# A second feed-forward bias as one more row of the down projection, with a new order table for the layers

## The reference

```python
xn = _layernorm(x)
x = x + _L0_attn_ref(xn, ...) + _L0_ffn_ref(xn, ...)

def _layer(x, wqkv, qs, ksc, wo, lg, lb, w1, b1, w2, b2):   # two of these, one after the other
    h = shift_token(x)                # second half of the columns comes from the token before
    ...                               # q, k, v; l2 norm; rotary tables; windowed attention
    x = x + o @ wo
    h = shift_token(x)
    h = (h - mu) / jnp.sqrt(var + 1e-05) * lg + lb
    h = h @ w1 + b1                   # 256 -> 2 * 682
    a, g = jnp.split(h, 2, axis=-1)
    h = a * jax.nn.gelu(g, approximate=False)
    x = x + h @ w2 + b2               # 682 -> 256; b2 is the bias that the change moves
    return x
```

## Time and profile before

| | us |
|---|---|
| three runs | 1958.6, 1950.5, 1962.69 |
| median | 1958.6 |
| the profiled execution | 1963.61 |
| its span, first to last instruction | 1961.8 |
| TensorE busy (matmul) | 1842.9, 94% of the span |
| ScalarE / VectorE / GpSimd busy | 1376.9 / 1246.3 / 922.5 |
| mean granted TensorE clock | 0.981 |

### The profile page before, as it was taken

The page is one execution under the profiler, slowest core; times in us unless marked ns, Lnnn a source line. Parts: engine busy times, 40 slices in busy tenths (PEclk is TensorE's granted clock), DMA queues, the critical chain, the costliest instruction groups (busy, mean ns, idle before and its releaser), DMA issues.

```text
span 1961.8 us, 47822 instructions
## 1 busy us (share of the span) xinstructions
PE 1842.9 (94%) x17808; PEld 1567.0 (80%) x17808; DVE 1246.3 (64%) x4125; ACT 1376.9 (70%) x3997; POOL 922.5 (47%) x1315
## 2 busy tenths in 40 slices
PE   6999999999999689999999999999999999999998
PEld 4788788788788469788788897887888878878777
DVE  4544543454443367777777777677777777777765
ACT  5886987878688365866757758667576585775764
POOL 2533543444344454636536446355364563654632
PEclk9999999999999889999999999999999999999999
DMA  4321320322324610110110101304112112010110
GB/s 146 99 76 56 116 87 34 116 76 77 88 78 146 196 41 23 47 55 23 47 43 24 55 15 53 122 15 166 39 39 63 34 47 65 25 54 25 44 45 28
DMA packets 127003, 128.91 MB, mean 66 GB/s; under 512 B 28112, under 2 KB 101940, under 8 KB 126772
## 3 DMA queue, kind: packets, MB, share of 16 engines
q1 hardware_dynamic: 123604, 119.56, 19.7%
q10 hardware_dynamic: 3168, 6.29, 0.9%
HBM read 72.84 MB, written 37.25 MB: 56 GB/s over the span
## 4 chain that ended last, share of the span: by engine, by line
PE 41%; DVE 11%; ACT 11%; issue 1%; POOL 1%; DMA 1%; SPq 0%; DVEq 0%; ACTq 0%; POOLq 0%
PE f_bank L1415 17%; PE f_bank L1552 7%; PE f_o_bank L1527 4%; PE f_scores L1567 4%; PE f_scores L1494 3%; ACT f_prob L1649 3%; DVE f_u L1803 3%; DVE f_gu L1799 2%; PE f_bank L1505 2%; ACT f_u L1669 2%; PE f_bank L1466 2%; PE f_bank L1509 1%; ACT f_probT L1590 1%; DVE f_actT L1688 1%; ACT f_probT L1594 1%
## 5 line engine op out<-in xcount | busy, mean ns | idle before, releaser
L594 POOL TENSOR_SCALAR a_prob<-a_prob,a_row_inv,a_gate 128x128 f32<-128x128 f32 x512 | 227.6, 468 | 377.7 <-DVE a_row_inv L932 377.7
L1370 POOL TENSOR_SCALAR f_prob<-f_prob,f_row_inv 128x192 f32<-128x192 f32 x512 | 214.5, 443 | 291.6 <-DVE f_row_inv L1745 291.6
L1415 PE MATMUL f_bank<-weights,f_actT 128*128 128x512 f32 x1152 | 302.9, 409 | 5.4 <-DVE f_norm L1693 3.9
L1552 PE MATMUL f_bank<-f_hT,f_w 128*128 128x256 f32 x2112 | 270.2, 283 | 5.4 <-DVE f_gu L1799 5.4
L1552 PEld LDWEIGHTS f_bank<-f_hT,f_w 128*128 128x128 f32 x2112 | 259.4, 189 | 10.3 <-DVE f_gu L1799 8.9
L1415 PEld LDWEIGHTS f_bank<-weights,f_actT 128*128 128x128 f32 x1152 | 211.7, 193 | 55.4 <-DVE f_norm L1693 7.7
L1352 POOL TENSOR_TENSOR f_qk_tok<-f_qk_tok,tables 128x512 f32<-128x512 f32 x128 | 165.1, 1313 | 158.4 <-DVE f_sin_part L1705 158.4
L1649 ACT ACTIVATE f_prob<-f_scores,f_neg_max 128x192 f32<-128x192 f32 x512 | 208.5, 428 | 14.1 <-DVE f_neg_max L1737 12.8
L1346 POOL TENSOR_TENSOR f_norm<-f_norm,f_minus_half 128x16 f32<-128x16 f32 x64 | 199.3, 3115 | 34.0 <-DVE f_norm L1697 32.4
L1669 ACT ACTIVATE f_u<-f_gu 128x256 fp32r<-128x256 f32 x192 | 80.3, 418 | 191.2 <-DVE f_gu L1799 191.2
L824 ACT ACTIVATE a_prob<-a_scores,a_neg_max 128x128 f32<-128x128 f32 x512 | 179.9, 392 | 24.0 <-DVE a_neg_max L923 17.0
(11 more groups left out here) (139 smaller groups left out, 3988.8 us busy)
## 6 DMA issues: line engine op xcount, KB each, us to landing
split_weights<-a_hi_lo SPq DMA_DIRECT2D x16, 512.0 KB
x_next<-states SPq DMA_DIRECT2D x32, 256.0 KB, 4.4
tables<-scaled_tables SPq DMA_DIRECT2D x16, 512.0 KB, 5.4
f_x<-states SPq DMA_DIRECT2D x16, 512.0 KB, 3.8
split_weights<-a_hi_lo SPq DMA_DIRECT2D x12, 682.0 KB
weights<-split_weights ACTq DMA_DIRECT2D x6, 1024.0 KB, 9.9
f_w<-split_weights SPq DMA_DIRECT2D x4, 1280.0 KB, 10.6
f_v_crossed<-f_v SPq DMA_DIRECT2D x40, 128.0 KB, 2.3
```

The costliest lines, as they stand in the source:

```text
L594: last = nc.gpsimd.tensor_scalar(part, part, row_inv[:, a % 2, head, t:t + 1], gate[:, half, t, h:h + 1], ALU.mult, ALU.mult)
L1370: last = nc.gpsimd.tensor_scalar(part, part, row_inv[:, a % 2, head, t:t + 1], 1.0, ALU.mult, ALU.mult)
L1415: last = nc.tensor.matmul(out, lhs(c, a), rhs(c, b), start=(i == 0), stop=(i == len(order) - 1))
L1552: mm = nc.tensor.matmul(out[:, which * PART:(which + 1) * PART], w1[:, wp, c, col:col + P], hT[:, hp, c, columns_of(a // FH)], start=(i == ...
```

## The change

The bias b2 becomes row 43 of the last block (`HR = HL + 1`). Its weight row in w2 is b2 itself, as high and low part. Its activation is 1: the gate's bias in that row is 8 (`UNIT_GATE`), whose gelu is 8, and the value's bias is 1/8. Both constants are written into `rows` by memsets. The steps `x1_bias` go, on GpSimd and in the semaphores. b2 is split in the attention phase (one ScalarE and one VectorE instruction on a tile of 2 x 512, a load and a store). `ORDER` is another table, in which also `load_x` stands ahead of `load_x1`, and `load_wqkv` after `("rope", 3)` and not at the end. The attention phase's last iteration has no `rows_in` and `rows_out` any more. The bookkeeping of semaphore values is written anew (`Count`), and TensorE waits for weights only where they are new.

```diff
+HR = HL + 1
+UNIT_GATE = 8.0
 # attention phase
         last = [(kind, a) for kind, a in steps if not (kind in A_PREPARE and a == HALVES - 1 or ...)
+                and kind not in ("rows_in", "rows_out")]
 # SP
+            sp.dma_start(bias[:], rows_in[2]).then_inc(bias_loaded, 16)
...
+                        if it == 0:
+                            sp.wait_ge(bias_split, 1)
+                            sp.dma_start(split_bias, bias_hi_lo[:].bitcast(F32)).then_inc(bias_stored, 16)
 # GpSimd
-            pool.memset(rows[:], 0.0)
+            gate_col, value_col = 3 * D + FH - 1, ROWS - 1
+            pool.memset(rows[:, 0:gate_col], 0.0)
+            pool.memset(rows[:, gate_col:gate_col + 1], 1.0 / UNIT_GATE)
+            pool.memset(rows[:, gate_col + 1:value_col], 0.0)
+            pool.memset(rows[:, value_col:ROWS], UNIT_GATE)
 # ScalarE and VectorE, once (it == 0 and a == 0)
+                            act.wait_ge(bias_loaded, 16)
+                            nc.scalar.activation(bias_hi_lo[:, HI, :], bias[:], ACT.Copy).then_inc(bias_hi, 1)
...
+                            nc.vector.tensor_tensor(bias_hi_lo[:, LO, :], bias[:], bias_hi_lo[:, HI, :].bitcast(F32), ALU.subtract).then_inc(bias_split, 1)
 # layers phase, the table (two of its lines)
-ORDER = [("softmax", 0), ("scores", 0), ("scores", 1), ("weigh", 0), ("weigh", 1), ("softmax", 1), ("load_x1", 0), ("transpose_x", 0),
...
+ORDER = [("softmax", 0), ("softmax", 1), ("scores", 0), ("scores", 1), ("weigh", 0), ("scores", 2), ("weigh", 1), ("transpose_x", 0),
...
+                sp.dma_start(w2[HL:HR, :, FH - 1, :].bitcast(F32), bias_in[layer].unsqueeze(0)).then_inc(w2_loaded, 16)
 # GpSimd
-                    elif kind == "x1_bias":
-
-                        pool.wait_ge(ln_scaled.sem, ln_scaled.past(it, ("ln_apply", 2 * a + 1)))
...
-                        nc.gpsimd.tensor_tensor(x1[:], x1[:], b2_row.unsqueeze(1).broadcast_to([P, TILES, D]), ALU.add).then_inc(x1_biased.sem, 1)
...
+                    pool.wait_ge(ln_scaled.sem, ln_scaled.past(it, ("ln_apply", 2 * a + 1)))
 # TensorE, prepare()
                     if a % TILES == 0:
-                        pe.wait_ge(kept.weights_loaded[QUERY], loads(1, layer))
-                        pe.sem_inc(pe_carried, 1)
+                        if fresh:
+                            pe.wait_ge(kept.weights_loaded[QUERY], loads(1, layer))
+                            pe.sem_inc(pe_carried, 1)
 # VectorE, low part of the last block
-                        place = u[0:m, a % GATED, LO, :] if j < FH - 1 else u[STACKED, a % GATED, HI, :]
-                        nc.vector.tensor_tensor(place, gu[0:m, a % 2, :], u[0:m, a % GATED, HI, :].bitcast(F32),
+                    low, place = (m, u[0:m, a % GATED, LO, :]) if j < FH - 1 else (HL, u[STACKED, a % GATED, HI, :])
+                    nc.vector.tensor_tensor(place, gu[0:low, a % 2, :], u[0:low, a % GATED, HI, :].bitcast(F32),
```

More of the change, by code:

```diff
@@ L740, in iteration @@
                         gates_back(it, a)
-            for it in range(0, BATCH - 1):
-                iteration(it, steps if it else opening)
-            iteration(BATCH - 1, last)
+            for each in tables:
+                iteration(*each)
         def high_targets(it, kind, a):
@@ L995, in layers_phase @@
+def layers_phase(nc, kept, attended_end, states, attended, out, wqkv_in, wo_in, w1_in, w2_in, bias_in, rows_in, tables_in, masks):
     with ExitStack() as ctx:
@@ L1062, in layers_phase, with layer_of @@
                   ("transpose_qk", t0 + 3)]
+        program = flat([(None, before), *((it, steps) for it in range(SEQUENCES - 1)), (SEQUENCES - 1, last)])
+        def layer_of(it):
+            return 1 if it is not None and it >= BATCH else 0
         def sem(name):
```

656 lines of the change are left out of this document (306 added, 350 removed).

## The result

| | before | changed |
|---|---|---|
| median of 20 runs, us | 1957.95 | 1961.66 |
| lowest and highest, us | 1950.5, 1962.69 | 1957.79, 1968.15 |
| the profiled execution, us (span) | 1963.61 (1961.8) | 1963.38 (1961.3) |

The ratio is 1.0023, with an interval of 1.0014 to 1.0032: 4.5 us slower. The forecast was 1943.8, and 1961.66 lies outside its range. Most of the terms that I had summed did arrive, one of them larger than I had it. What ate them is in a place for which I had written zero.

A forecast was written before the change was run, and what follows sets the result against it. TensorE's matmuls were taken to bound each chunk, so only its waits and clock count. Terms -5.0 -7.4 -3.9 -3.0 +1.5 +3.0 = -14.8 us gave 1943.8 us for the median, range 1929 to 1959.

The forecast's parts named there:

- the passage: From attention phase to layers: without the seven loads and the rows store, TensorE starts 5.0 us earlier.
- GpSimd's additions: Layer 1: one bias addition fewer slows VectorE's subtraction, so TensorE's 7.4 us of gate-product waits go; bounds 0 and 7.4.
- the last chunk: End of the layers: without the addition, ln_apply's second step ends 2.2 us earlier and 1.7 of clock loss goes, gain 3.9.
- the rest of the change: Row 43, bias split and about 32 dropped TensorE weight waits: counted as 0, bounds -1.5 and +1.5 us.
- the change of layers: Weights' change between layers: loads issued a third of a chunk earlier gain 3.0 us, bounds 0 and 3.5.
- the order at a chunk's start: scores 2 ahead of transpose_x: wait grows to 1.9 us, mostly made up; 0.1 in each of 15 chunks, +1.5 us.
- the order in the middle: Middle of each chunk: the prediction found the new order to change nothing there and gave it no term.
- The prediction's own falsifier: Signs against it: start wait over 2.3 us, transpose 1 over 0.83 later, or new mid-chunk waits over 0.5 per chunk.
- rival 3: Chunk start: longer wait not made up, transposes 1.5 us later per chunk, clock falls in all fifteen; 1969, chance 0.1.
- The clock: Chunk starts: two of the four at full clock fall too, 13 or so of 15 near 0.79; +3 us.

The follow-up runs named there:

- passage alone: Kernel before, only with rows_in and rows_out dropped from the attention phase's last iteration: 1955.83 us, ratio 0.9975.
- additions left out: Kernel before with the short passage, GpSimd's sixteen additions of bias b2 left out and the bias added nowhere: 1935.17 us, ratio 0.9888.
- old table: Changed kernel with the ORDER table of before, without x1_bias; bias row, short passage and new bookkeeping stay: 1933.12 us, ratio 0.987.
- loads moved: Changed kernel with the table of before, load_x put ahead of load_x1 and load_wqkv behind rope 3: 1930.55 us, ratio 0.9851.
- new start in the old table: Changed kernel with the table of before, only scores 2 moved ahead of weigh 1 and transpose_x: 1940.96 us, ratio 0.9904.
- rope_sum 1 shortened: Changed kernel, new table kept, VectorE's addition and product in rope_sum 1 on one head of eight: 1937.41 us, ratio 0.9887.
- old kernel with the values first: Kernel before, values 0 and 1 moved ahead of scores 4 and take_o 0 ahead of softmax 3: 1974.65 us, ratio 1.0078.

## Why the prediction was wrong, point by point

| step | predicted | measured | by |
|---|---|---|---|
| the passage | -5.0 | -4.9 | passage alone |
| GpSimd's additions, with the last chunk | -7.4 -3.9 | -17.0 | additions left out against passage alone |
| the rest of the change, in the old table | 0 | -3.5 | old table against additions left out |
| the change of layers | -3.0 | -3.7 | loads moved against not |
| the order at a chunk's start, with its clock | +1.5 +3.0 | +6.7 | new start in the old table |
| the order in the middle | 0 | +26.6 | new table against rope_sum 1 shortened |
| sum | -14.8 | +4.1 | changed kernel: +4.5 |

The measured column is made of differences of ratios times 1958, so single entries are uncertain by 3 to 6 us. One sum of them is a real check: the loads (-3.7) and the new start (+6.7) on top of the old table give 0.9885, and the new table without its meeting has 0.9887. It is good to about 8 us. The windows at full clock say the same, 1.55 to 1.65 per chunk for the middle.

**The failed step is "where I found the order to change nothing", in the middle of the chunk.** I had compared the lists of the engines there and seen that TensorE's and GpSimd's steps in front of `transpose 7` were in nearly the same order. They are. What changed is when VectorE's steps fall against GpSimd's. The trace of before had it all: GpSimd's chain without a pause, a norm at 3.95 where others take 2.91, and TensorE at `transpose 7` with 0.2 us to spare or less. I had used the same mechanism for the bias addition and did not ask where else it stands. The prediction's own falsifier, new waits of over 0.5 us per chunk in the middle, is what came. My term for this step was 0; it is +26.6 us by the ratios, and 1.55 to 1.65 us per chunk at full clock.

The Trainium skill, SBUF — State Buffer, SBUF: two separate sides, has a pair of ports that VectorE and GpSimd can only hold one at a time, each for a whole instruction; a VectorE instruction with two inputs in SBUF needs the pair when GpSimd's instruction reads SBUF, and so does one in a two-port mode. The traces agree: the addition to `f_x`, with one input in PSUM, runs beside `weigh 6` before, which takes 1.66; the rotary sum and product, with two inputs in SBUF, make it 3.61.

**GpSimd's additions.** The mechanism was right, the size was not. Layer 1's gate waits went from 7.4 to 1.0, and at full clock the additions cost 1.15 per chunk there, 8 us in seven. The last chunk, from its first score matmul to the end, took 69.4 us in the passage alone and 66.1 without the additions, 3.3 where I had 3.9. But I gave layer 0 nothing, since its listed waits were 0.7 us, and the slow subtraction stood in the earlier trace rows; there it is 0.6 per chunk, 5 us in eight. Laid side by side matmul for matmul, a first half of layer 0 with and without the addition parts by 0.4 us at the last `up` steps and by 0.3 at the last `down` steps, a second half by 0.2 and 0.3. Those are waits of a tenth of a microsecond between matmuls, which the profile counts as busy. The changed kernel in the old table gains another 0.3 in the second halves, at the second `transpose_h`. No addition stands there, and which edit gives it stays open.

**The chunk's start.** I wrote that `transpose 1` ends where it did or 0.3 later, and took 0.1. From the first matmul of `scores 0` to that of `scores 3` it is 8.61 us in the chunk of the earlier trace rows, and 8.72 after. But that chunk of before was at the lower clock from 1105.1 on, which stretched its transposes. At full clock the old order takes 7.94 (the old table, chunk from 1087.3), so the cost is 0.78. What I set against the new order was a baseline slowed by the clock; my term of 0.1 per chunk should have been 0.8, 12 us over fifteen. What holds TensorE there is what rival 3 named: the low parts, which VectorE does behind the masks of `scores 2`, and for which TensorE waits up to 0.7 us at a time. Rival 3 put its threshold at 0.83 per chunk, where with the clock it eats the gains; it did not get there alone.

**The clock.** I expected 13 of 15 starts to fall; in the profiled execution nine did. The term of +3.0 had the wrong sign here. Its price was wrong too. I took 1.7 us for each stretch of 3.4 us at 0.50, as if TensorE were busy all through it. The rows show less. Before, six chunks with one stretch each take 78.5 us on average, and the same order of layer 0 at full clock, in the passage alone, 77.4: 1.1 each. In the changed kernel six chunks with three stretches take 79.05 and a pair without one takes 79.0 each: next to nothing. Laid side by side, the chunk from 943.0 with a stretch is up to 0.96 us behind the one from 1101.3 without one, over `transpose_x` and `transpose 0`, and has made it all up at the end of `transpose 1`: the stretch falls just ahead of the waits for VectorE's low parts and GpSimd's second product, and these become shorter. This gives back part of the 12 us that the new start costs at full clock, which fits the +6.7 by the ratios. Before, the stretches in layer 0 began at 791.1, 869.6, 948.1, 1026.6, 1105.1 and 1183.7: 78.5 us apart, about a chunk's length. In the old kernel with the values first they were nearly gone, and it was 15 us slower all the same.

**The passage** came in size, -4.9 for -5.0. In the changed kernel the tables landed 5.6 us behind their issue at 653.20, and TensorE began 0.1 behind that and not 0.64.

**The change of layers** came in size, 2.2 us at full clock (79.3 against 77.1) or 3.7 by the ratios, for 3.0. That the chunk itself went from 82.0 to 79.1 was partly luck. Before, its granted clock was 0.96 and now it is 1.00; the additions are gone from it, and the new order's waits have come into it.

**The last chunk** had a term of its own wrong. The wait of 3.17 falls to 1.0 where the additions are left out in the old order (0.99 in the passage without them, 1.00 in the old table), as worked out. In all five kernels with the new table it is 1.8. So the new order costs 0.8 us there, where I had put nothing. That `up 2` ahead of the second layer norm is what does it is likely, but no run moves it alone.

One reading is off without consequence: 5.4 us in 15 waits over eight chunks are 0.68 per chunk, not 0.75.

## What to carry to other kernels

When a table of order changes, comparing each engine's list is not enough where two engines slow each other down. Mark in the old trace every engine that works without a pause up to the moment another one needs it, and every instruction that lasts longer than its like; here a shift of 0.8 us decided who meets whom. And test the parts of a change apart: here a new order of steps worth +33 us hid edits and moved loads worth -29, and the version with the old table and the loads moved runs at 1930.55, below both kernels.

## What I had not expected of the hardware

- Waits too short to be listed added up to 0.5 us per chunk. TensorE's busy time for two chunks was 149.20 with the addition and 148.20 without, for the same matmuls.
- A stretch of 3.4 us at the lower clock cost 1.1 us in the old order and next to nothing in the new one, where it falls just ahead of waits of TensorE.
- A meeting moved from one GpSimd instruction to another does not cost the same: the norms took 1.04 us longer beside `rope_sum 1` (3.95 for 2.91), four `weigh` pieces 1.95 longer (3.61 for 1.66).
- A wait can be put down to an engine that ended at the same moment by chance, 1138.62 against 1138.58.
- Taking a wait of 0.27 us from TensorE cost 0.9 us further on in each first half, since VectorE's step then came 0.4 us earlier against GpSimd's chain (`weigh 6` at 2.64 for 1.62).
